# Attention beside a mixture of experts: score operands stored once, transfers two at a time, work moved off VectorE

## The chip, the core and the metric

The kernel runs on one core of a Trainium2 chip. The metric is the device time of one execution in microseconds; a profiled execution adds a span (first to last instruction) and a trace. TensorE, VectorE, ScalarE and GpSimd compute; SP only issues DMAs. All float data is fp32.

## The reference

x has 8 batches of 512 rows of 128 channels. It is normalised (xn), and the output is x + attention(xn) + experts(xn).

```python
q, k, v = (xn @ w.T + b  for wq, wk, wv)          # 16 heads of 8 channels
scores  = where(xn[:, :, 0] != 0, q k^T * 8**-0.5, -inf)
att     = softmax(scores) @ v @ wo.T + bo

logits  = xn @ gate_w                              # 4096 rows, 8 experts
top 2 per row, router_probs = softmax of the two
rank of each (choice, row) within its expert; kept if rank < 1280
slots   = kept rows of xn, gathered by (expert, rank)
y       = gelu(slots @ c_fc[e] + fc_bias[e]) @ c_proj[e] + proj_bias[e]
ffn     = sum over the two choices of weight * y[slot]
```

## The kernel before, in words

Every engine runs a list of instructions written out by hand; semaphores are the only order between engines. The stages are these.

**Front.** For each of the 8 batches the rows are normalised (VectorE), transposed (TensorE), and multiplied by the weights of q and k. Both are split into a high part, rounded to the fast fp32 format of TensorE (`high` on ScalarE), and a low part, the rest (`late` on VectorE). The score product is then formed from 24 rows per head: K's (low, high, high) against Q's (high, high, low), three rows for each of 8 channels. `write_stacks` on SP stores these triples to `q_rows` and `k_rows` in HBM, with four DMAs a batch; a high part may be overwritten two batches later only when its stores have landed (`s_wr`). GpSimd adds the bias of v and stores a mask row to `k_rows`.

**Preparation.** VectorE picks the two best experts; GpSimd turns ranks into slots (`put_i`, `get_i`, weights `wgt`). TensorE meanwhile forms the first scores for the maxima and, between them, filler products (`keep_clock`). GpSimd then adds the output bias to `acc` in one instruction, fills `slot_x` with zeros by ten DMAs, one at a time, and scatters the rows of xn to their slots by 64 indirect DMAs, each released at a group of attention (`put_after`).

**Attention.** A batch has 16 groups: two units of 8 heads, each as two quads of 4 heads, times 4 blocks of 128 keys. In a group TensorE forms four transposed scores (line 967), each followed by an exponential on ScalarE (line 621), four products of the group before with v (line 983), and, eight groups ahead, two pairs of scores (line 948) whose row maxima VectorE takes (line 765). Every four groups, here called a quarter, SP loads the stacks of one quad of the next batch (`load_quad`, 8 DMAs) and, behind them on the same queue, writes the maxima of a quad into rows of Q (`max_rows`, 4 DMAs); these were turned by TensorE in the second group of a quarter and are needed at the first group of the next. In the first groups of a batch the previous batch is normalised, turned, projected with wo (line 1002) and added to `acc` (`take_out`).

**Experts.** They run after four groups of batch 4. For each expert TensorE turns the slot rows `xe` (line 991), forms the first product from split parts (lines 1059 to 1063) and the second (line 1074), with the turning of the next expert's rows woven in as `BETWEEN` says: two chunks of rows, a result, the last chunk of rows, two results. VectorE writes `ye`, SP stores it to `slot_y`. SP's order per expert is: wait for the rows of e to be split, load rows of e + 1, wait for the results of e, store them, load the weights of e + 2.

**Combining.** GpSimd gathers each row's two results from `slot_y` by 64 indirect DMAs, again released at groups (`got_after`). Batches 0 to 3 are combined by GpSimd, 4 to 6 by VectorE between maxima (line 830, at the groups in `COMBINED_AT`), batch 7 by VectorE at the end. SP writes each batch out.

## Time and profile before

| | us |
|---|---|
| median of 3 runs | 714.14 |
| lowest, highest | 707.48, 723.22 |
| profiled execution | 716.14 |
| its span | 714.3 |
| TensorE busy | 618.3 (87%) |
| VectorE busy | 406.7 (57%) |
| ScalarE busy | 394.9 (55%) |
| GpSimd busy | 229.0 (32%) |
| chain that ended last | TensorE 52%, VectorE 21%, DMA 8%, ScalarE 6% |

The profile divides the span by engine and by line. A busy share says little about what bounds, since matmuls overlap in the array; the waits (who sat idle, and what ended that) and the chain of work that ended last say more. The granted clock of TensorE has two levels here, 1.2 and 2.4 GHz, shown as 0.5 and 1.0 of full speed.

### The profile page before, as it was taken

How to read it: one execution, taken by the hardware profiler on the slowest of the kernel's cores; microseconds unless marked ns; L12 is line 12 of the kernel's file. 1: busy time of each engine (PE TensorE's matmuls, PEld its weight loads, DVE VectorE, ACT ScalarE, POOL GpSimd, SP SyncE). 2: the span in 40 equal slices, each digit the busy share in tenths (PEclk: the TensorE clock that was granted, in tenths of full speed). 3: DMA queues.
4: the chain of work that ended last, by engine and by line, in shares of the span. 5: the costliest groups of instructions: out<-in, count | busy, mean ns of one | idle time of the engine just before them, and what ended most of it. 6: DMA issues, size and time to landing. Idle time of an engine off the chain costs nothing.

```text
span 714.3 us, 9757 instructions
## 1 busy us (share of the span) xinstructions
PE 618.3 (87%) x3526; PEld 322.6 (45%) x3526; DVE 406.7 (57%) x601; ACT 394.9 (55%) x775; POOL 229.0 (32%) x230
## 2 busy tenths in 40 slices
PE   4767999599999999989778867969999999899884
PEld 2433443223333343358767766869334333224312
DVE  5758598458888979831111110111798988857602
ACT  3442067357778877883144134323877787655751
POOL 3856911623343431200110011010255566322310
PEclk9989599759999999999789989889999999756955
DMA  6887044211212121422133033211312122111120
GB/s 191 248 277 233 21 180 155 72 38 51 73 54 74 59 68 39 119 67 74 34 107 104 27 84 108 64 45 38 102 47 76 48 73 80 58 43 27 47 66 15
DMA packets 57999, 60.44 MB, mean 85 GB/s; under 512 B 8032, under 2 KB 42848, under 8 KB 57952
## 3 DMA queue, kind: packets, MB, share of 16 engines
q1 hardware_dynamic: 52160, 45.92, 21.3%
q0 software_dynamic: 5792, 13.90, 6.3%
q8 instruction: 28, 0.46, 0.3%
q14 instruction: 19, 0.16, 0.1%
HBM read 29.65 MB, written 29.62 MB: 83 GB/s over the span
## 4 chain that ended last, share of the span: by engine, by line
PE 52%; DVE 21%; DMA 8%; ACT 6%; SPq 5%; issue 4%; POOL 1%; another core or an unknown queue 1%; DVEq 0%; POOLq 0%; ACTq 0%
DVE nmax L765 14%; PE bPV L983 14%; PE bX L967 12%; PE bD L1074 12%; DMA xe<-slot_x 5%; PE bD L948 5%; ACT probs L621 4%; PE bPV L1109 2%; PE bX L957 2%; DMA k_rows<-hid 2%; PE bD L991 1%; PE bD L1002 1%; DVE ye L808 1%; SPq L368 1%; DVE attn L783 1%
## 5 line engine op out<-in xcount | busy, mean ns | idle before, releaser
L765 DVE TENSOR_REDUCE nmax<-bD 128x2 f32<-128x1024 f32 x256 | 300.5, 1218 | 76.5 <-PE bD L948 58.7
L621 ACT ACTIVATE probs<-bX 128x512 f32<-128x512 f32 x512 | 268.2, 597 | 114.7 <-PE bX L967 102.6
L967 PE MATMUL bX<-Q,K 27*128 27x512 f32 x512 | 186.4, 503 | 19.0 <-ACT probs L621 12.6
L983 PE MATMUL bPV<-probs,v_aug 128*32 128x512 f32 x1024 | 152.0, 668 | 1.6 <-ACT probs L621 0.7
L967 PEld LDWEIGHTS bX<-Q,K 27*128 27x128 f32 x512 | 76.0, 196 | 163.5 <-ACT probs L621 111.3
L948 PE MATMUL bD<-K,Q 25*128 25x512 f32 x512 | 137.2, 508 | 10.7 <-DVE nmax L765 7.4
L1074 PE MATMUL bD<-wpj,hid 128*128 128x128 f32 x640 | 88.2, 306 | 11.4 <-DVE xeT_lo L798 6.3
L1074 PEld LDWEIGHTS bD<-wpj,hid 128*128 128x128 f32 x640 | 85.8, 220 | 14.8 <-issue 14.8
L512 POOL DMA_INDIRECT slot_x<-xn_all,put_i x64 | 62.4, 975 | 90.3 <-PE bPV L983 76.4
L649 ACT ACTIVATE hid<-bX,fcb 128x512 f32<-128x512 f32 (+1 forms) x96 | 55.5, 615 | 47.1 <-PE bX L1063 46.5
L948 PEld LDWEIGHTS bD<-K,Q 25*128 25x128 f32 x512 | 58.6, 197 | 47.1 <-DVE nmax L765 29.8
L519 POOL TENSOR_TENSOR wfc_hi<-wfc,ones 128x512 fp32r<-128x512 f32 x8 | 10.1, 1265 | 175.4 <-DMA pjb<-in_pjb 175.4
L808 DVE TENSOR_TENSOR ye<-bD,pjb 128x512 f32<-128x512 f32 (+1 forms) x24 | 14.5, 603 | 84.2 <-PE bD L1074 84.2
L798 DVE TENSOR_TENSOR xeT_lo<-bD,xeT_hi 128x512 fp32r<-128x512 f32 (+1 forms) x24 | 13.9, 597 | 80.1 <-ACT xeT_hi L646 80.1
L542 POOL DMA_INDIRECT xn_all<-slot_y,get_i x32 | 32.2, 1005 | 69.8 <-PE bPV L983 65.1
L542 POOL DMA_INDIRECT hid<-slot_y,get_i x32 | 32.0, 999 | 64.7 <-PE bPV L983 54.9
L646 ACT CAST xeT_hi<-bD 128x512 fp32r<-128x512 f32 (+1 forms) x24 | 11.9, 517 | 67.5 <-PE bD L991 67.5
L983 PEld LDWEIGHTS bPV<-probs,v_aug 128*32 128x32 f32 x1024 | 21.3, 112 | 38.9 <-ACT probs L621 23.2
L1059 PE MATMUL bX<-xeT_hi,wfc_lo 128*128 128x512 f32 (+1 forms) x96 | 35.1, 366 | 0.7 <-ACT hid L649 0.7
L1063 PE MATMUL bX<-xeT_lo,wfc_hi 128*128 128x512 f32 (+1 forms) x96 | 34.2, 357 | 0.0
L1060 PE MATMUL bX<-xeT_hi,wfc_hi 128*128 128x512 f32 (+1 forms) x96 | 34.1, 355 | 0.0
L991 PE MATMUL bD<-ident,xe 128*128 128x128 f32 x80 | 14.5, 323 | 22.5 <-DMA xe<-slot_x 21.5
(104 smaller groups left out, 488.3 us busy)
## 6 DMA issues: line engine op xcount, KB each, us to landing
K<-k_rows SPq DMA_DIRECT2D x128, 50.0 KB
Q<-q_rows SPq DMA_DIRECT2D x128, 48.0 KB
slot_x<-hid POOLq DMA_DIRECT2D x10, 512.0 KB, 3.0
xe<-slot_x SPq DMA_DIRECT2D x8, 640.0 KB, 6.3
slot_y<-ye SPq DMA_DIRECT2D x8, 640.0 KB, 4.3
q_rows<-hid SPq DMA_DIRECT2D x8, 512.0 KB, 3.7
k_rows<-hid SPq DMA_DIRECT2D x8, 512.0 KB, 5.4
acc<-in_x SPq DMA_DIRECT2D x8, 256.0 KB, 4.9
```

The lines of the kernel that those rows point to most:

```text
L512: pool.indirect_dma_start(slot_x, bass.IndirectOffsetOnAxis(ap=put_i[:, col:col + 1], axis=0), xn_all[:, n, :], None, bounds_check=SLOTS - ...
L542: pool.indirect_dma_start(gathered(b, k * TT + n), None, slot_y, bass.IndirectOffsetOnAxis(ap=get_i[:, col:col + 1], axis=0), bounds_check ...
L621: taken(nc.scalar.activation(probs[:, (g % 2) * 4 + i, :], next_x()[:], ACT.Exp, scale=SCALE))
L649: taken(nc.scalar.activation(hid[:, hc, c0:c0 + w], next_x()[:, 0:w], ACT.Gelu, bias=fcb_s[q][:, hc:hc + 1]))
L765: nc.vector.tensor_reduce(nmax[q][:, k, 2 * pair:2 * pair + 2], bank()[:], AX.X, ALU.max, negate=True).then_inc(s_dd, 1)
L948: last = nc.tensor.matmul(to[:, n, :], Q[u][rows_used, q, k * P:(k + 1) * P], K[u][rows_used, q, :], start=True, stop=True)
L967: filled(nc.tensor.matmul(next_x()[:], K[u][rows_used, q, j * P:(j + 1) * P], Q[u][rows_used, q, :], start=True, stop=True))
L983: last = nc.tensor.matmul(bPV[32 * h:32 * h + 32, :], v_aug[b % 2][:, j, u * UH + QUAD * q + h, :], probs[:, (g % 2) * 4 + h, :], start=(g ...
L1059: nc.tensor.matmul(to, lo, xeT[0][:, c0:c0 + w], start=True, stop=False)
L1060: nc.tensor.matmul(to, hi, xeT[0][:, c0:c0 + w], start=False, stop=False)
L1063: filled(nc.tensor.matmul(to, hi, xeT[1][:, c0:c0 + w], start=False, stop=True))
L1074: last = nc.tensor.matmul(to[:, 0, k * P:(k + 1) * P], hid[:, hc, c0 + k * P:c0 + (k + 1) * P], wpj[e % 2][:, hc, :], start=(hc == 0), sto ...
```

## The change

Eight things change. (1) `q_rows` and `k_rows` hold, for each channel, one high and one low row; two stores a batch write them, and `load_quad` makes the triples by reading the high row of Q twice: four DMAs a head instead of two. (2) The stores of batches 0 to 5 stand ahead of the first load. (3) Zero stores, scatters and gathers wait for the one two before them, on a pair of semaphores, and for no group. (4) The output bias is added in eight pieces, one after every second of the first sixteen scatters. (5) SP loads the rows of expert e + 2 ahead of the wait for the results of e. (6) Batches 4 to 6 are combined by GpSimd behind the last gather. (7) The first filler row on TensorE after the ranks has 8 products instead of 3. (8) In the last eight groups, where no scores for maxima are left, TensorE forms two pairs of score products that nobody reads.

```diff
-HI, LO = (1, 0), (0, 1)
+HI, LO = 1, 0
...
-COMBINED_BY_POOL = 4
+COMBINED_BY_POOL = 7
 N_CONST, N_LATER = 8, 3
-WR_DMAS, LOAD_DMAS, MAX_DMAS = 4, 8, 4
+WR_DMAS, LOAD_DMAS, MAX_DMAS = 2, 16, 4
...
+def taken_out(b):
+
+    return D_FIRST + (b + 1) * D_TURN + (E * D_EXPERT if b > EXPERTS_AFTER else 0)
...
-        q_rows = nc.dram_tensor("q_rows", [B, H, ROW_MASK, T], F32, kind="Internal").ap()
-        k_rows = nc.dram_tensor("k_rows", [B, H, ROW_MAX, T], F32, kind="Internal").ap()
+        q_rows = nc.dram_tensor("q_rows", [B, H, DH, 2, T], F32, kind="Internal").ap()
+        k_rows = nc.dram_tensor("k_rows", [B, H, DH + 1, 2, T], F32, kind="Internal").ap()
...
                 sp.wait_ge(s_lo, b * 2 + 2)
                 for w, stack in ((0, q_rows), (1, k_rows)):
-                    three = stack[b, :, 0:ROW_MASK, :].rearrange("h (c r) t -> h c (r t)", r=3)
-                    sp.dma_start(three[:, :, 0:2 * T], parts[w, q].rearrange("p s t -> p (s t)")).then_inc(s_wr[b], 16)
-                    sp.dma_start(three[:, :, 2 * T:3 * T], parts[w, q][:, HI[w], :]).then_inc(s_wr[b], 16)
+                    sp.dma_start(stack[b, :, 0:DH].rearrange("h c s t -> h c (s t)"), parts[w, q].rearrange("p s t -> p (s t)")
+                                 ).then_inc(s_wr[b], 16)
 
             def load_quad(b, u, q):
 
@@ -333,9 +326,13 @@
                     sp.wait_ge(s_wr[b], WR_DMAS * 16)
                     sp.wait_ge(s_wm[b % 2], b // 2 * 16 + 16)
                 for h in range(QUAD):
-                    for tile, stack, n in ((Q[u], q_rows, ROW_MASK), (K[u], k_rows, ROW_MAX)):
-                        sp.dma_start(tile[STRIP * h:STRIP * h + n, q, :].bitcast(F32), stack[b, h0 + h]
-                                     ).then_inc(s_load[u][q], 16)
+                    at = STRIP * h
+                    for start, stop, tile, src in (
+                            (0, 2 * DH, Q[u], q_rows[b, h0 + h, :, HI, :][None, :, :].to_broadcast([2, DH, T])),
+                            (2 * DH, ROW_MASK, Q[u], q_rows[b, h0 + h, :, LO, :]),
+                            (0, 2 * DH, K[u], k_rows[b, h0 + h, 0:DH].rearrange("c s t -> s c t")),
+                            (2 * DH, ROW_MAX, K[u], k_rows[b, h0 + h, :, HI, :])):
+                        sp.dma_start(tile[at + start:at + stop, q, :].bitcast(F32), src).then_inc(s_load[u][q], 16)
 
...
-            for b in range(3):
+            for b in range(B - 2):
                 write_stacks(b, b % 2)
             sp.wait_ge(s_ones, 2 * UNITS)
             load_quad(0, 0, 0)
-            for b in range(3, 6):
-                write_stacks(b, b % 2)
+            write_stacks(B - 2, 0)
+            write_stacks(B - 1, 1)
             load_quad(0, 0, 1)
-            for b in range(6, B):
-                write_stacks(b, b % 2)
-                load_quad(0, 1, b % 2)
+            for q in range(2):
+                load_quad(0, 1, q)
...
             def experts():
-                sp.wait_ge(s_put, KN * 16)
+                for q in range(2):
+                    sp.wait_ge(s_put[q], KN // 2 * 16)
                 load_rows(0)
+                sp.wait_ge(s_dd, rows_item(0, NCH - 1) + 1)
+                load_rows(1)
                 for e in range(E):
-                    if e < E - 1:
-                        sp.wait_ge(s_dd, rows_item(e, NCH - 1) + 1)
-                        load_rows(e + 1)
+                    if e + 2 < E:
+                        sp.wait_ge(s_dd, rows_item(e + 1, NCH - 1) + 1)
+                        load_rows(e + 2)
                     sp.wait_ge(s_dd, results_end(e))
                     sp.dma_start(slot_y_v[e], ye[:]).then_inc(s_slot, 16)
...
-                    take_pool(2, COMBINED_BY_POOL)
+                    take_pool(2, 4)
...
+            take_pool(4, COMBINED_BY_POOL)
...
-            pool.wait_ge(s_xn, B)
-            nc.gpsimd.tensor_tensor(acc[:], acc[:], bo_s[:, None, :].to_broadcast([P, NT, C]), ALU.add).then_inc(s_bo, 1)
             pool.wait_ge(s_fill, 7)
             for h in range(ZERO_DMAS):
                 pool.dma_start(slot_x.rearrange("(p h r) c -> h p (r c)", p=P, h=ZERO_DMAS)[h], hid_f[:, 0:per]
-                               ).then_inc(s_zero, 16)
-                pool.wait_ge(s_zero, h * 16 + 16)
+                               ).then_inc(s_zero[h % 2], 16)
+                wait(pool, s_zero[1 - h % 2], (h + 1) // 2 * 16)
+            pool.wait_ge(s_xn, B)
+            pool.wait_ge(s_zero[(ZERO_DMAS - 1) % 2], ZERO_DMAS // 2 * 16)
             for k in range(TOPK):
                 for n in range(NT):
                     col = k * NT + n
-                    pool.wait_ge(s_pv, put_after(col))
+                    wait(pool, s_put[col % 2], col // 2 * 16)
                     pool.indirect_dma_start(slot_x, bass.IndirectOffsetOnAxis(ap=put_i[:, col:col + 1], axis=0),
                                             xn_all[:, n, :], None, bounds_check=SLOTS - 1, oob_is_err=False
-                                            ).then_inc(s_put, 16)
+                                            ).then_inc(s_put[col % 2], 16)
+                    if col < 2 * B and col % 2 == 1:
+                        b = col // 2
+                        nc.gpsimd.tensor_tensor(rows(acc, b), rows(acc, b), bo_s[:, None, :].to_broadcast([P, TT, C]),
+                                                ALU.add).then_inc(s_bo, 1)
             for e in range(E):
...
+                for q in range(2):
+                    pool.wait_ge(s_get[b][q], TOPK * TT // 2 * 16)
+                pool.wait_ge(s_dd, taken_out(b))
...
-                        pool.wait_ge(s_pv, got_after((b * TOPK + k) * TT + n))
+                        if k * TT + n >= 2:
+                            pool.wait_ge(s_get[b][n % 2], (k * TT + n) // 2 * 16)
+                        elif b > 0:
+                            pool.wait_ge(s_get[b - 1][n % 2], TOPK * TT // 2 * 16)
                         pool.indirect_dma_start(gathered(b, k * TT + n), None, slot_y,
                                                 bass.IndirectOffsetOnAxis(ap=get_i[:, col:col + 1], axis=0),
-                                                bounds_check=SLOTS - 1, oob_is_err=False).then_inc(s_get[b], 16)
-                        if 0 < b <= COMBINED_BY_POOL and (k, n) == (0, 2):
+                                                bounds_check=SLOTS - 1, oob_is_err=False).then_inc(s_get[b][n % 2], 16)
+                        if 0 < b <= EXPERTS_AFTER + 1 and (k, n) == (0, 2):
                             combine(b - 1)
+            for b in range(EXPERTS_AFTER + 1, COMBINED_BY_POOL):
+                combine(b)
...
-                dve.wait_ge(s_bo, 1)
+                dve.wait_ge(s_bo, b + 1)
...
-                if b * GB + g in COMBINED_AT:
-                    combine(COMBINED_AT[b * GB + g])
...
+            def unused_products():
+
+                to = free()
+                for n in range(2):
+                    at = STRIP * n
+                    nc.tensor.matmul(to[:, n, :], Q[1][at:at + NR_MAX, 1, 0:P], K[1][at:at + NR_MAX, 1, :], start=True, stop=True)
...
+                    else:
+                        unused_products()
...
-                        keep_clock(3)
+                        keep_clock(8 if (s, pair) == (2, 0) else 3)
```

Three places show what moves. On SP, at the start of the experts; `xe` are slot rows, `ye` results, the rest weights. Before:

```order
L345 DMA Q<-nmT 2x512 x4
L363 DMA xe<-slot_x 128x10x128 x2
L380 DMA slot_y<-ye 128x10x128
L367 DMA wfc<-in_c_fc 128x512
L368 DMA wpj<-in_c_proj 128x4x128
L369 DMA fcb<-in_fcb 128x4
L370 DMA pjb<-in_pjb 128x128
L363 DMA xe<-slot_x 128x10x128
L380 DMA slot_y<-ye 128x10x128
```

After:

```order
L342 DMA Q<-nmT 2x512 x4
L359 DMA xe<-slot_x 128x10x128 x3
L379 DMA slot_y<-ye 128x10x128
L363 DMA wfc<-in_c_fc 128x512
L364 DMA wpj<-in_c_proj 128x4x128
L365 DMA fcb<-in_fcb 128x4
L366 DMA pjb<-in_pjb 128x128
L359 DMA xe<-slot_x 128x10x128
L379 DMA slot_y<-ye 128x10x128
```

The load of the third expert's rows now stands ahead of the first store of results, and so on for each expert.

On VectorE, batch 6, groups 6 to 10; `nmax` are row maxima, line 830 the combine. Before:

```order
L771 TENSOR_TENSOR nmhl<-nmax,nmhl 128x16
L765 TENSOR_REDUCE nmax<-bD 128x2 x4
L779 RECIPROCAL rsum<-bD 128x32
L783 TENSOR_TENSOR attn<-bD,rsum 128x4x32 x2
L830 SCALAR_TENSOR_TENSOR acc<-hid,wgt,acc 128x128 x8
L765 TENSOR_REDUCE nmax<-bD 128x2 x4
L770 CAST nmhl<-nmax 128x16
L771 TENSOR_TENSOR nmhl<-nmax,nmhl 128x16
```

After:

```order
L784 TENSOR_TENSOR nmhl<-nmax,nmhl 128x16
L778 TENSOR_REDUCE nmax<-bD 128x2 x4
L792 RECIPROCAL rsum<-bD 128x32
L796 TENSOR_TENSOR attn<-bD,rsum 128x4x32 x2
L778 TENSOR_REDUCE nmax<-bD 128x2 x4
L783 CAST nmhl<-nmax 128x16
L784 TENSOR_TENSOR nmhl<-nmax,nmhl 128x16
```

The combine is gone from between the maxima.

On TensorE, the last batch, around its eighth group; `bX` takes scores for exponentials, `bD` scores for maxima. Before:

```order
L983 MATMUL bPV<-probs,v_aug 32x512 x4
L967 MATMUL bX<-Q,K 128x512
L957 MATMUL bX<-ident,nmhl 8x128 x4
L967 MATMUL bX<-Q,K 128x512 x3
L983 MATMUL bPV<-probs,v_aug 32x512 x4
L991 MATMUL bD<-ident,pv_s 128x128 x4
L967 MATMUL bX<-Q,K 128x512 x4
L983 MATMUL bPV<-probs,v_aug 32x512 x4
```

After:

```order
L1003 MATMUL bPV<-probs,v_aug 32x512 x4
L987 MATMUL bX<-Q,K 128x512
L977 MATMUL bX<-ident,nmhl 8x128 x4
L987 MATMUL bX<-Q,K 128x512
L970 MATMUL bD<-K,Q 128x512 x2
L987 MATMUL bX<-Q,K 128x512
L970 MATMUL bD<-K,Q 128x512 x2
L987 MATMUL bX<-Q,K 128x512
L1003 MATMUL bPV<-probs,v_aug 32x512 x4
L1011 MATMUL bD<-ident,pv_s 128x128 x4
L987 MATMUL bX<-Q,K 128x512 x2
L970 MATMUL bD<-K,Q 128x512 x2
```

Each group has two pairs of products more, in the places that the scores for maxima have in earlier groups.

## Rows read from the trace of the kernel before

**Rows 1.** The page, section 2: granted clock in 40 equal slices

```profile
PEclk9989599759999999999789989889999999756955
```

**Rows 2.** Waits, whole run: total us, times, longest us

```profile
PEld bD L991 <- DMA xe<-slot_x: 22.8, 6, 4.1
...
ACT hid L557 <- DMA k_rows<-hid: 20.9, 6, 5.1
...
ACT probs L621 <- remote: 6.8, 2, 6.4
```

**Rows 3.** Timeline of the front, ScalarE and GpSimd: start us, us, what [idle before]

```profile
21.43 0.69 ACT L557 ACTIVATE hid<-bX,bq_s 128x512 fp32r<-128x512 f32 x1 [1.73 <-DMA k_rows<-hid]
...
54.39 0.69 ACT L557 ACTIVATE hid<-bX,bq_s 128x512 fp32r<-128x512 f32 x1 [2.33 <-DMA k_rows<-hid]
...
30.18 1.92 POOL L446 TENSOR_SCALAR mrow<-ye 1x512 fp32r<-1x512 f32 x1
...
34.34 1.92 POOL L446 TENSOR_SCALAR mrow<-ye 1x512 fp32r<-1x512 f32 x1
```

**Rows 4.** Timeline of the preparation, TensorE: filler products between pairs

```profile
80.07 1.65 PE L1109 MATMUL bPV<-hot,ones_r 128*128 128x512 f32 x3
...
82.37 1.65 PE L1109 MATMUL bPV<-hot,ones_r 128*128 128x512 f32 x3
...
89.33 0.96 PE L1109 MATMUL bPV<-hot,ones_r 128*128 128x512 f32 x3
...
90.64 0.96 PE L1109 MATMUL bPV<-hot,ones_r 128*128 128x512 f32 x3
```

**Rows 5.** Timeline of TensorE, experts 0 and 1

```profile
319.22 1.04 PE L991 MATMUL bD<-ident,xe 128*128 128x128 f32 x8
...
326.23 5.60 PE L1074 MATMUL bD<-wpj,hid 128*128 128x128 f32 x48 [0.73 <-DVE ye L808]
...
342.51 1.97 PE L991 MATMUL bD<-ident,xe 128*128 128x128 f32 x8 [3.70 <-DMA xe<-slot_x]
```

**Rows 6.** The chain of waits: start us, us, what

```profile
260.05 1.10 PE bD L1002 x8
...
307.39 1.09 PE bD L1002 x8
...
362.52 6.29 DMA xe<-slot_x
...
479.31 5.60 PE bD L1074 x48
...
547.15 1.10 PE bD L1002 x8
...
657.15 1.10 PE bD L1002 x8
```

**Rows 7.** Timeline of VectorE, batch 6

```profile
614.06 2.31 DVE L830 SCALAR_TENSOR_TENSOR acc<-hid,wgt,acc 128x128 f32<-128x128 f32 x8
```

**Rows 8.** Timeline of TensorE, last batch

```profile
680.15 1.94 PE L983 MATMUL bPV<-probs,v_aug 128*32 128x512 f32 x8
...
684.21 1.94 PE L983 MATMUL bPV<-probs,v_aug 128*32 128x512 f32 x8
```

**Rows 9.** Timeline of SP's queue, two quarters of batch 2

```profile
237.03 0.30 SPq L337 DMA_DIRECT2D Q<-q_rows  x1
...
248.05 0.29 SPq L337 DMA_DIRECT2D Q<-q_rows  x1
...
250.44 0.30 SPq L337 DMA_DIRECT2D K<-k_rows  x1
251.84 2.41 SPq L345 DMA_DIRECT2D Q<-nmT  x4
```

**Rows 10.** DMA queues, 213.9 to 224.9 us (one quarter): packets, MB, share

```profile
q1 hardware_dynamic: 280, 0.42, 11.8%
```

**Rows 11.** DMA issues: count, KB each, median us to landing

```profile
bk_s<-in_bk SPq DMA_DIRECT2D x1, 0.5 KB, 2.1
```

29 lines of the change are left out of this document (13 added, 16 removed).

## The prediction

> **What bounds the kernel now.** I read the page's slices first, then the waits, then the chain that ended last, and at each place where the chain names something other than TensorE or the maxima on VectorE, the timeline there. The clock slices [rows 1] say where to look: TensorE's granted clock is at its upper level, 2.4 GHz, in most slices and falls to half, 1.2 GHz, in the preparation (slice 5), in slices 8 and 9, in a part of every expert (the 7 and the 8s of slices 20 to 27), and in five of the last six. A group of attention costs 11.0/4 = 2.76 us at the upper level ([rows 9]: loads of consecutive quarters start at 237.03 and 248.05) and 4.06 us at the lower [rows 8], because TensorE then needs longer than the two maxima on VectorE. So a short pause of TensorE costs its own length and then 1.3 us per group until the clock is back. Three pauses are visible: the exponentials that wait for stored stacks in the front, the expert rows that wait for their load [rows 2], and one pause of 6.4 us on an unnamed releaser near 135 us [rows 2].
>
> **The change, part by part.** The sum is made against the profiled execution, 716.1 us (span 714.3, 1.8 outside it), which lies 2.0 over the median of the runs.
>
> *Front.* Stores shrink from four DMAs of 1,536 KB per batch to two of 1,024 KB, and no load stands between them before batch 5. ScalarE waited 20.9 us in six waits for a store two batches back [rows 2]; the high parts of batches 2 and 7 are 54.39 − 21.43 = 32.96 us apart, 6.6 per batch [rows 3]. Without that wait the next limit is GpSimd's mask, store and bias of a batch, 34.34 − 30.18 = 4.16 us [rows 3]. Five intervals at 4.16 are 20.8 us: a gain of at most 12. Against it, the first load is now issued behind six batches and takes sixteen DMAs, so it may reach TensorE up to 5 us after the front's end. I take **−8**, bounds −12 and −3.
>
> *Preparation.* TensorE runs 12 pairs of score products after the ranks, at 82.37 − 80.07 = 2.30 us a pair at the lower clock, and at 90.64 − 89.33 = 1.31 at the upper [rows 4]. Ahead of the first it now issues 8 filler products instead of 3: three take 1.65 us [rows 4], so 5 more take 2.8. If this denser stretch of work lifts the clock after two or three pairs, 9 pairs save 1.0 us each, −9 + 2.8 = −6.2; if not, +2.8. No row shows eight in a row from this state; I take **−3.5**, the middle, leaning to a gain, since in the experts the clock came back each time once full 128-row products ran.
>
> *GpSimd's queue.* The bias of the output (acc plus bo) leaves its place ahead of the zero stores and is cut in eight pieces among the first sixteen scatters; zero stores and scatters go two at a time, held only by their own landing. The scatters had been spread over four batches, so that without the spreading they end long before the experts read the slots; each of the eight pieces precedes its take-out by many groups. TensorE waits for none of it: **0**. The pause near 135 us falls into a run of scatters issued back to back, but its releaser is not named; I leave it at 0, bounds −15 (6.4 of pause, some 2 of slow issue before it, and five groups that then ran at 4.06, 5 × 1.3) and +15 (a second such).
>
> *Experts.* This is the largest term. SP issues the next load of expert rows behind the last result, its store and four weight loads; it takes 6.29 us [rows 6], and TensorE, done with the first products, waits 3.70 us [rows 5], six times, 22.8 us [rows 2]. After each the clock falls. Periods: the last 12 chunks of results start at 326.23 [rows 5] and 479.31 [rows 6], so (479.31 − 326.23)/6 = 25.5 us. An undisturbed period is built from the same rows: 326.23 − 319.22 = 7.0 (rows to the second result) plus 342.51 − 3.70 − 326.23 = 12.6 (results and first products) = 19.6. The load now goes out once the third chunk of rows is split, ahead of the last two results; these and the first products, the 12.6 us above, cover 6.3. (25.5 − 19.6) × 6 = **−36**. If the clock fell all the same, the pauses alone give −22. Cover: if a load took over 12 us, TensorE would wait again. What is late next is the weight split on GpSimd, which has a whole expert of time.
>
> *Combines on VectorE.* Three leave VectorE for GpSimd's end. The one at 614.06 takes 2.31 us [rows 7] between maxima; TensorE's banks are full, and the clock stays low for ten groups. Batches from 260.05 to 307.39 take 47.3; two from 547.15 to 657.15 take 110.0 [rows 6]: 110.0 − 94.7 = **−15.3**. All of it should return, as nothing else stands there. On GpSimd three combines of four passes each run behind the last gather, and only batch 6's has to wait for a take-out, which comes 12 groups before the end: hidden.
>
> *Unused products.* In the last eight groups TensorE repeats the score pairs for nobody. It fell to 4.06 us per group at about 680 [rows 8]; five groups at 2.76 give −6.5, and the closing transposes and projection, all at the lower clock too, perhaps −2. Cost of the added products: in all other groups they fit in 2.76. **−8.5**, bounds 0 and −11.
>
> *Loads.* Each quarter's load becomes 16 DMAs on SP instead of 8, and the maxima rows (4 DMAs) stand behind them. Eight take 250.44 − 248.05 + 0.30 = 2.7 us, 0.34 each; the maxima's four are issued in 2.41 [rows 9], and a small DMA lands 2.1 after issue [rows 11]. From the load's first issue T, the maxima rows land at T + 16 × 0.34 + 1.8 + 2.1 = T + 9.3; TensorE needs them a quarter later, T + 11.0. Cover 1.7 us, so **0**. Bounds: the issue cost of the new shapes is between 0.34 and the 0.60 of the maxima's two-row DMAs (2.41/4); from 0.44 on, TensorE waits.
>
> How many engines a load uses can be read off its small packets: in one quarter 280 packets of which 204 are rows [rows 10]; the other 76 are 4 × 12 + 4 × 5 + 4 × 2, so 24 rows went over 12 engines, 25 over 5, 2 over 2. The Trainium skill, DMA: Bandwidth & Descriptors, "Why a DMA increments its semaphore by 16 and not by 1", gives the rule: the count is the largest number up to 16 that divides the slowest dimension of both sides, on the lowest-numbered engines; by it the two new 16-row forms, whose slowest dimension is 2, would use two engines. By that rule the trace agrees for the old shapes; for the new ones (16 rows twice over 2, 8 over 8, 9 over 9) it would put 4 × (8 + 8 + 1 + 1) = 72 rows of a quarter on each of two engines, against 28 so far, with the maxima rows behind them, and the cover of 1.7 would shrink to about nothing. The sum stands without it.
>
> Sum: −8 − 3.5 − 36 − 15.3 − 8.5 = −71.3; 716.1 − 71.3 = **645 us**.
>
> **Rivals.** (a) *The pause near 135 us goes too*: 645 − 15 = 630. For it: the scatters beside it had no wait on a landing; against: scatters land fast enough that two in flight is the same pace. (b) *Maxima rows late by about 1 us* in each of the 31 quarters, clock unharmed: 645 + 31 = 676. For it: the 1.7 us of cover, and GpSimd's transfers, now at full pace beside them. (c) *Slower: the same wait drops the clock.* From an issue cost over 0.44 us, TensorE pauses at each quarter's head; where the pause comes near the 2.3 us of the combine [rows 7], the shortest that a fall followed, a batch runs some 12 of 16 groups at 4.06: 96 low groups in place of the 20 of before (5, 10 and 5 above), 76 × 1.3 = +99, and 716 − 47.5 + 99 = 768. A low clock makes the quarter long enough for the loads, so it settles there and no deeper. (d) *The change does not hold the clock*: the fillers bring +2.8 and the unused products nothing: 645 + 6.3 + 8.5 = 660. For it: no row shows score products alone bringing a fallen clock back; against: the full attention groups consist mostly of them and keep the upper level.
>
> **How the numbers follow.** The forecast 0.58, (a) 0.13, (b) 0.12, (c) 0.09, (d) 0.08. The forecast's own bounds are 630 to 662. The range goes from 622 (a and a better front) to 690 (b with some fallen clocks); only (c) and a little beyond lie outside. A measurement of this kernel can tell about 2% from no change: under 700 faster, over 728 slower. Faster 0.84, same 0.06, slower 0.10.
>
> **What would show it.** In the changed profile: no wait on the expert rows' load, and a clock slice of 9 through the experts, one in 19 to 20 us; high parts 4 to 5 us apart in the front; no low clock in the last three batches; the maxima rows' last issue no later than 8 us after their quarter's first load. Wrong would be: waits of the score products on the maxima rows, load issues of 0.45 us or more, or low slices inside the attention batches, which say (b) or (c); 2.30 us pairs to the end of the preparation, which say (d).

## The result, and the profile after

The change makes the kernel **slower**: 765.6 us median (754.3 to 775.3), against 713.1 of before, ratio 1.068 (95% interval 1.047 to 1.088). The profiled execution took 764.1 us, its span 762.3. Ratios here compare quick executions with quick ones, since a clock that falls by chance makes single executions longer; medians and ranges are given beside them, and the kernel before always ran on the same chip.

The clock slices come first again, from the page of the changed kernel (section 2):

```profile
PEclk9989655569559657855999999999556855977996
```

Against [rows 1], the experts (slices 20 to 28) are all 9 now, and the attention before and behind them is at 5 and 6 in long stretches where it was 9. So one part gave what it should, and something else took far more. The waits of the changed kernel (total us, times, longest us) name it:

```profile
PE bX L987 <- DMA Q<-nmT: 22.2, 7, 10.2
...
ACT hid L570 <- DMA k_rows<-hid: 6.8, 4, 2.7
```

TensorE waits for the maxima rows, which it never did before; the wait on `xe` [rows 2] is gone, and the wait for a store in the front fell from 20.9 to 6.8 us. Seven waits of 22 us in all don't make the 48 us by which the span grew. What they do is seen where one ends. SP's queue and TensorE at the head of the third quarter of batch 3, two timelines of the changed kernel:

```profile
304.02 1.09 SPq L335 DMA_DIRECT2D Q<-q_rows  x2
305.15 1.08 SPq L335 DMA_DIRECT2D K<-k_rows  x2
...
312.92 2.42 SPq L342 DMA_DIRECT2D Q<-nmT  x4
315.38 1.09 SPq L335 DMA_DIRECT2D Q<-q_rows  x2
```

```profile
313.50 1.07 PE L1003 MATMUL bPV<-probs,v_aug 128*32 128x512 f32 x8
314.49 0.50 PE L987 MATMUL bX<-Q,K 27*128 27x512 f32 x1
316.51 0.49 PE L987 MATMUL bX<-Q,K 27*128 27x512 f32 x1 [1.52 <-DMA Q<-nmT]
316.95 0.43 PE L987 MATMUL bX<-Q,K 27*128 27x512 f32 x2
317.31 1.94 PE L1003 MATMUL bPV<-probs,v_aug 128*32 128x512 f32 x8
```

Two things are to be seen here. The first is the cost of an issue, the time that SP spends on starting one DMA: a pair takes 1.09 us, and the next starts 0.04 later, so 0.56 an issue, where [rows 9] had 0.34. Sixteen take 8.9 us and the maxima's four 2.4, so SP is busy for 11.3 us of a quarter that lasts 11.0 at the upper clock. The maxima rows land 1.1 us after their last issue, at 316.5, 12.5 after the quarter's first load. TensorE had been ready at 315.0. The second is the clock: behind the pause of 1.52 us the eight products with v take 1.94 us instead of 1.07, so it has fallen.

In batches 1 to 6 it fell in this way at the head of the third quarter, and once more at the head of batch 7, behind a pause of 1.57 us at 697.1. In batch 0 it was low from the start, behind the wait of 10.2 us. In batch 1 the pause is 1.16 us and the table names no releaser for it; it ends at 187.3, 1.1 us behind the last maxima issue, as the others do. In batches 1 to 5 the clock came back only at the next batch's head, with its products of 128 rows; batch 6 fell at 669.5 and had it back at 677.7, behind such products too. Batch lengths, from the first score product of one batch to that of the next (us):

| | b0 | b1 | b2 | b3 | b4 with experts | b5 | b6 |
|---|---|---|---|---|---|---|---|
| before | 55.9 | 51.2 | 47.3 | 47.4 | 239.7 | 47.3 | 57.0 |
| after | 67.5 | 65.1 | 64.5 | 64.3 | 222.5 | 64.5 | 57.5 |

The front and the preparation, ScalarE and TensorE of the changed kernel:

```profile
20.81 0.69 ACT L570 ACTIVATE hid<-bX,bq_s 128x512 fp32r<-128x512 f32 x1 [1.08 <-PE bX L902]
...
42.55 0.69 ACT L570 ACTIVATE hid<-bX,bq_s 128x512 fp32r<-128x512 f32 x1 [2.69 <-DMA k_rows<-hid]
```

```profile
50.29 0.80 PE L961 MATMUL bD<-K,Q 25*128 25x512 f32 x4 [7.46 <-DMA K<-k_rows]
...
59.71 2.11 PE L1130 MATMUL bPV<-hot,ones_r 128*128 128x512 f32 x8 [0.73 <-ACT wpj L601]
...
64.29 0.96 PE L1130 MATMUL bPV<-hot,ones_r 128*128 128x512 f32 x3
65.18 0.50 PE L961 MATMUL bD<-K,Q 25*128 25x512 f32 x2
65.61 0.96 PE L1130 MATMUL bPV<-hot,ones_r 128*128 128x512 f32 x3
...
77.83 1.20 PE L1130 MATMUL bPV<-hot,ones_r 128*128 128x512 f32 x4
89.19 0.79 PE L987 MATMUL bX<-Q,K 27*128 27x512 f32 x1 [10.17 <-DMA Q<-nmT]
```

High parts of batches 2 and 7 are now (42.55 − 20.81)/5 = 4.35 us apart instead of 6.6 [rows 3]. The preparation runs at 1.32 us a pair from its start, where [rows 4] had 2.30 for the most part, and is done at 79.0. Then TensorE waits 10.2 us, because the first maxima rows stand behind 64 load issues on SP.

The experts, chain of waits (start us, us, what), the last twelve chunks of results:

```profile
385.79 5.60 PE bD L1096 x48
405.21 5.60 PE bD L1096 x48
...
482.90 5.60 PE bD L1096 x48
```

The period is (482.90 − 385.79)/5 = 19.4 us, against 25.5 [rows 5], [rows 6]. The spans can be compared by segments. The attention starts at 89.2 instead of 93.1: −3.9. From the last products with v ahead of the experts to the first behind them it is 159.1 instead of 195.7: −36.6. All other attention takes 514.0 instead of 425.5: +88.5. Together that is +48.0, by which the spans differ.

### The profile page after: what moved, and what is told of

It reads as the page before. It is cut to its first block, busy times and chain, and to the rows that moved or that the text cites. A ratio compares the mean times of both kernels' runs of the same rounds, so it can differ in the third digit from the quotient of the medians.

```text
span 762.3 us, 10070 instructions
## 1 busy us (share of the span) xinstructions
PE 674.6 (88%) x3563; PEld 319.2 (42%) x3563; DVE 403.5 (53%) x577; ACT 396.0 (52%) x775; POOL 244.3 (32%) x249
## 4 chain that ended last, share of the span: by engine, by line
PE 64%; ACT 13%; DVE 9%; SPq 7%; issue 4%; DMA 2%; DVEq 0%; ACTq 0%
PE bPV L1003 22%; PE bX L987 19%; PE bD L1096 10%; ACT hid L662 6%; SPq L335 5%; ACT probs L634 5%; PE bD L961 4%; DVE nmax L778 4%; PE bX L977 3%; PE bD L1011 2%; DMA Q<-nmT 2%; SPq L342 1%; PE bD L1022 1%; DVE xn_all L713 1%; DVE hid L722 1%
## 5 line engine op out<-in xcount | busy, mean ns | idle before, releaser
L987 PE MATMUL bX<-Q,K 27*128 27x512 f32 x512 | 224.3, 615 | 35.5 <-DMA Q<-nmT 22.2
L1003 PE MATMUL bPV<-probs,v_aug 128*32 128x512 f32 x1024 | 199.0, 861 | 0.8 <-ACT probs L634 0.7
L987 PEld LDWEIGHTS bX<-Q,K 27*128 27x128 f32 x512 | 92.8, 244 | 234.1 <-ACT probs L634 106.9
L961 PE MATMUL bD<-K,Q 25*128 25x512 f32 x512 | 150.0, 614 | 13.5 <-DMA K<-k_rows 7.5
L1096 PE MATMUL bD<-wpj,hid 128*128 128x128 f32 x640 | 74.9, 277 | 13.5 <-DVE xeT_lo L811 8.4
L1096 PEld LDWEIGHTS bD<-wpj,hid 128*128 128x128 f32 x640 | 72.6, 192 | 16.4 <-issue 16.4
L961 PEld LDWEIGHTS bD<-K,Q 25*128 25x128 f32 x512 | 61.8, 247 | 34.9 <-issue 15.6
L1003 PEld LDWEIGHTS bPV<-probs,v_aug 128*32 128x32 f32 x1024 | 23.3, 126 | 48.0 <-ACT probs L634 26.0
L617 ACT CAST nmT<-bX 8x512 fp32r<-8x512 f32 x32 | 18.4, 574 | 21.4 <-PE bX L977 19.4
L977 PE MATMUL bX<-ident,nmhl 128*8 128x128 f32 x128 | 28.3, 365 | 0.1
```

The costliest lines, as they stand in the source:

```text
L961: last = nc.tensor.matmul(to[:, n, :], Q[u][rows_used, q, k * P:(k + 1) * P], K[u][rows_used, q, :], start=True, stop=True)
L977: last = nc.tensor.transpose(to[0:8, k * P:(k + 1) * P], nmhl[q][:, k, :, :].rearrange("p h s -> p (h s)").bitcast(F32), ident[:])
L987: filled(nc.tensor.matmul(next_x()[:], K[u][rows_used, q, j * P:(j + 1) * P], Q[u][rows_used, q, :], start=True, stop=True))
L1003: last = nc.tensor.matmul(bPV[32 * h:32 * h + 32, :], v_aug[b % 2][:, j, u * UH + QUAD * q + h, :], probs[:, (g % 2) * 4 + h, :], start=(g ...
L1096: last = nc.tensor.matmul(to[:, 0, k * P:(k + 1) * P], hid[:, hc, c0 + k * P:c0 + (k + 1) * P], wpj[e % 2][:, hc, :], start=(hc == 0), sto ...
```

## The experiments

Each kernel is given by its difference from another. "On old stacks" means the first one below. The letters of theories and rivals are those of the expectations.

### Is it the loads?

**Old stacks.** All of the change, but the layout, stores and loads of before (part 1 undone):

```diff
-WR_DMAS, LOAD_DMAS, MAX_DMAS = 2, 16, 4
+WR_DMAS, LOAD_DMAS, MAX_DMAS = 4, 8, 4
...
-                            (0, 2 * DH, Q[u], q_rows[b, h0 + h, :, HI, :][None, :, :].to_broadcast([2, DH, T])),
...
+                    for tile, stack, n in ((Q[u], q_rows, ROW_MASK), (K[u], k_rows, ROW_MAX)):
+                        sp.dma_start(tile[STRIP * h:STRIP * h + n, q, :].bitcast(F32), stack[b, h0 + h]
```

> The changed kernel with the operand stacks of the kernel before: triples stored, eight loads of 24 and 25 rows a quarter. Theory A (SP's issue time: sixteen issues at 0.55 us and the maxima's four take 11.3 us of a quarter of 11.0, TensorE pauses at the quarter's head and its clock falls): the load's issues go back to 2.7 us a quarter, no wait on the maxima rows, batches of 47.3 us, and the other seven parts keep what they bring: 645 to 655. Rival B (the unpaced scatters and gathers, or the combines at GpSimd's end, slow the transfers or TensorE): batches stay well over 50 us and the time over 690.

Measured: 658.5 us median (642.5 to 660.2; before, on this chip, 715.9). No wait on the maxima rows is left; batches 2, 3, 5 and 6 take 47.3 to 48.0. Batch 0 ran at the lower clock throughout in the profiled execution, 66.8 us, from 86.8 on and with no pause of TensorE of 0.3 us or more in the 8 us ahead, which the page shows as slices 6 to 10:

```profile
PEclk9988965555999999999999999999999999999997
```

**The loads alone**, on the kernel before:

> The kernel before with the new stacks and their sixteen loads alone. Theory A: batches of some 64.5 us as in the changed kernel, and none of the other gains: the changed kernel's 765 plus 36.6 of the experts plus some 8 of the last groups, 800 to 815. Rival B: the loss needs the unpaced transfers, so this one stays within 2% of 714.

Measured: 814.7 us (804.0 to 820.1), ratio 1.135 (1.115 to 1.155). Seven waits again, and batches of 62 to 69 us, with the scatters still spread as before:

```profile
PE bX L970 <- DMA Q<-nmT: 16.8, 7, 3.3
```

So part 1, the new layout with its stores and loads, is necessary and sufficient: with it alone the loss is there, and where it alone is undone the loss is gone.

**Pairs.** The sixteen rows channel by channel, so that K's lie in one piece:

```diff
-                            (0, 2 * DH, Q[u], q_rows[b, h0 + h, :, HI, :][None, :, :].to_broadcast([2, DH, T])),
+                            (0, 2 * DH, Q[u], q_rows[b, h0 + h, :, HI, :][:, None, :].to_broadcast([DH, 2, T])),
...
-                            (0, 2 * DH, K[u], k_rows[b, h0 + h, 0:DH].rearrange("c s t -> s c t")),
+                            (0, 2 * DH, K[u], k_rows[b, h0 + h, 0:DH].rearrange("c s t -> (c s) t")),
```

> The changed kernel with the sixteen rows of Q and K ordered channel by channel in pairs, so that K's sixteen rows lie in one piece in HBM. If the issue cost follows the pieces of the address pattern, K's sixteen-row issue falls from 0.60 to 0.30 and Q's stays at 0.61: mean pitch 0.48, the maxima rows land 16 x 0.48 + 3.6 = 11.3 us after the quarter's first load, 0.3 late. Theory A with a graded effect: pauses of 0.3 us, too short to cost the clock, about 655 to 665. Theory A with any pause costing the clock: 740 to 765. Rival C (two DMA engines carry the sixteen-row loads and hold up the maxima rows): the rows spread over more engines, maxima land sooner after their issue than 1.1 us and that alone mends it.

Measured: 716.7 us (688.7 to 726.3; before 715.9), between the two expectations. SP's timeline of that kernel, one quarter:

```profile
283.43 1.22 SPq L335 DMA_DIRECT2D Q<-q_rows  x2
284.69 0.69 SPq L335 DMA_DIRECT2D K<-k_rows  x2
...
290.57 1.96 SPq L335 DMA_DIRECT2D K<-k_rows  x2
292.58 2.46 SPq L342 DMA_DIRECT2D Q<-nmT  x4
```

K's pair of issues went from 1.08 to 0.69, Q's rose from 1.08 to 1.22. This quarter has one issue that is 1.3 us longer than its like, and such single long issues decide: the maxima rows landed at 296.2, 12.7 us after the first load and 1.2 after their own last issue. By rival C the number of DMA engines should have mattered. Here the form uses eight and sixteen of them, and a quarter has 365 packets where the changed kernel has 296; the rows landed as soon behind their last issue as in the changed kernel. So what was late was the issue, not the transfer.

The pause is graded, and its price is not. With the clock at the upper level ahead of it, pauses of 0.2 to 0.8 us at a quarter's head (four in this kernel, one in the next) left it there. The pauses from 1.2 to 3.3 us in the changed kernel, the loads alone and these two were 19; every one was followed by groups at the lower level, 12 of them to the end of the batch. Away from a quarter's head shorter pauses were followed by a fall too: 0.95 us in this kernel, at 186.0, and 0.68 and 0.77 in two kernels below.

**Old stacks, each load cut in two** plain DMAs of 12 and 12 or 13 rows:

```diff
+                        for start, stop in ((0, 12), (12, n)):
+                            sp.dma_start(tile[STRIP * h + start:STRIP * h + stop, q, :].bitcast(F32),
+                                         stack[b, h0 + h, start:stop]).then_inc(s_load[u][q], 16)
```

> The old stacks, but each load of 24 or 25 rows cut into two DMAs of 12 and 12 or 13 rows: sixteen DMAs a quarter of plain contiguous rows. Prediction's assumption (0.34 us an issue whatever the count) puts 5.4 + 3.6 = 9.1 us before the maxima rows are there, inside 11.0: time as with eight loads, 645 to 655. If the number of DMAs by itself costs (0.55 each even for plain rows): 750 to 770.

Measured: 707.8 us (689.7 to 721.1; before 715.9), so neither. This is the prediction's assumption built: sixteen plain loads. A pair of them takes 0.77 us, and now and then 1.0 more:

```profile
258.47 0.77 SPq L332 DMA_DIRECT2D Q<-q_rows  x2
259.28 1.79 SPq L332 DMA_DIRECT2D K<-k_rows  x2
261.11 2.41 SPq L340 DMA_DIRECT2D Q<-nmT  x4
```

At 0.41 an issue four batches kept their 47 to 52 us, but the 64 issues in the preparation made TensorE wait 4.1 us for the first maxima, and batches 0 and 1 then took 67.5 and 65.1. The fall in batch 1, at 194.1, isn't behind a maxima wait: it follows pauses of 0.51, 0.94 and 0.32 us without a named releaser, while GpSimd's scatters ran. By the medians (658 with eight plain loads, 708 with sixteen, 766 with sixteen of the new forms) the number of DMAs and their form each have a large part in the loss. Single executions of each kernel spread by 18 to 31 us, so the split is rough.

### What are the other parts worth?

**Three fillers** on old stacks (part 7 undone: `keep_clock(3)` everywhere):

> The changed kernel with the old stacks, and three filler products after the ranks instead of eight (part 7 undone). Theory D (the eight fillers bring the clock to its upper level for the preparation, but the attention that follows then loses it at its start and runs batch 0 at the lower level: 66.8 us instead of some 50): with three the preparation runs at 2.30 us a pair, batch 0 starts at the upper level as in the kernel before, and the time is 645 to 650 in every run, below the 658 of the run with old stacks alone. Rival E (batch 0's fall has nothing to do with the fillers): the preparation gets slower by some 6 us and batch 0 is low as often as before: 650 to 668.

Measured: 644.5 us (638.2 to 662.1), ratio 0.926 (0.908 to 0.943). The profiled execution started its attention 8 us later than with eight fillers (91.4 against 83.4) and ran batch 0 in 44.7. But one execution of four took 662, and a kernel with eight fillers (combines on VectorE, below) ran its batch 0 in 43.9. So theory D is not settled. In none of the four profiles with three fillers (the kernel before, the loads alone, this one, and the kernel before with two in flight) did batch 0 start low. With eight fillers and no wait for the first maxima it did in three of eleven. The execution of 662 has no profile, so where it lost its time isn't known.

**Fillers in the first groups** of batch 0, eight pairs of 128-row products on old stacks:

```diff
+                if b == 0 and LEAD <= u * UH + s < LEAD + 4:
+                    for n in range(2):
+                        nc.tensor.matmul(to[:, n, :], ones_r[:], hot_f, start=True, stop=True)
```

> The changed kernel with the old stacks, and two filler products of 128 rows ahead of each pair of score products in the first four groups of batch 0 (16 in all, whose results nobody reads). Theory F (batch 0 falls because its first groups have too little work in TensorE after the dense preparation, and full 128-row products keep or bring back the clock, as the turned sums did at the head of batch 1): batch 0 takes 50 to 55 us instead of 66.8, cost of the fillers some 2 to 4 us, 642 to 650 in every run. Rival: batch 0 low all the same, 660 to 665.

Measured: 642.4 us (639.0 to 648.5), ratio 0.929 (0.918 to 0.941), as theory F had it. It did not hold: see the same kernel again, below.

**Two in flight in the kernel before** (scatters held also by the landing of the one two before):

> The kernel before, with the 64 scatters held in addition by the landing of the one two before them; nothing else changed. Theory G (the pause of 6 us near 135 us comes from a dozen scatters issued back to back without a wait for a landing): no pause, batch 0 some 10 to 15 us shorter, time 700 to 706. Rival: the pause comes from something else at that place (it stays, or moves), and the time is that of the kernel before.

Measured: 700.0 us (694.3 to 718.1) against 704.5 (690.2 to 731.1), ratio 1.006 (0.999 to 1.013). In the profile the pause is gone and batch 0 takes 43.8 us instead of 55.9; the times show no gain. Since the kernel before itself ran in 690 here, its pause was perhaps not in every execution, or not at that price; no profile shows which.

**Combines on VectorE** again, on old stacks (part 6 undone):

> The changed kernel with the old stacks, but batches 4 to 6 combined by VectorE between maxima as in the kernel before (part 6 undone). By the prediction's term the three combines cost 15.3 us: 3 x 2.3 us at least, and a fallen clock after the one near the end: 658 plus 7 to 15. If the fall before was chance, plus 7 only or nothing.

Measured: 649.1 us (642.8 to 670.9), ratio 0.936 (0.922 to 0.950). VectorE and TensorE of that kernel where a combine stands:

```profile
555.87 2.32 DVE L844 SCALAR_TENSOR_TENSOR acc<-hid,wgt,acc 128x128 f32<-128x128 f32 x8
```

```profile
559.37 0.50 PE L963 MATMUL bD<-K,Q 25*128 25x512 f32 x2 [1.44 <-DVE nmax L778]
...
561.17 1.60 PE L1005 MATMUL bPV<-probs,v_aug 128*32 128x512 f32 x8
```

The same 1.4 us pause stood behind the combine near the end of the kernel before, where eight groups ran low behind it. Here the clock falls too, but for two groups only: the three groups from 556.43 to 569.65 take 13.2 us, against 8.4 in batch 5, so 4.9 more. A second combine at the head of batch 7 cost 2.7, the third nothing.

**No unused products**, on old stacks with the fillers in batch 0 (part 8 undone):

> The kernel with old stacks and fillers in batch 0's first groups, without the unused products of the last eight groups (part 8 undone). Theory H (they hold the clock to the end): the last four groups and the closing products run at the lower level, +6 to +9 us, 649 to 651. Rival: the clock holds or falls there either way, within 2 us of 642.

Measured: 674.4 us (660.2 to 683.2; before 712.9), ratio 0.936 (0.923 to 0.950). The time can't be read as expected, since batches 1 and 2 lost the clock on this chip without any quarter's wait. Both falls stand behind a pause of TensorE while scatters ran, 1.44 us at 148.0 and 0.68 at 206.7. At the first, ScalarE, VectorE and GpSimd went on within 0.05 us of one another (148.67 to 148.72), though the products that ScalarE is said to wait for had ended by 148.0. So the releasers named here need not be the cause:

```profile
148.67 2.15 ACT L631 ACTIVATE probs<-bX 128x512 f32<-128x512 f32 x4 [1.88 <-PE bX L987]
149.45 0.50 PE L961 MATMUL bD<-K,Q 25*128 25x512 f32 x2 [1.44 <-DVE acc L800]
```

The end can be read. TensorE's last products with v, of this kernel and of the changed one:

```profile
655.26 1.94 PE L1003 MATMUL bPV<-probs,v_aug 128*32 128x512 f32 x8
659.33 1.94 PE L1003 MATMUL bPV<-probs,v_aug 128*32 128x512 f32 x8
```

```profile
742.87 1.07 PE L1003 MATMUL bPV<-probs,v_aug 128*32 128x512 f32 x8
745.47 1.07 PE L1003 MATMUL bPV<-probs,v_aug 128*32 128x512 f32 x8
747.64 1.94 PE L1003 MATMUL bPV<-probs,v_aug 128*32 128x512 f32 x8 [0.69 <-ACT probs L634]
```

From the tenth group's products with v to the last it is 22.3 us here and 15.2 in the changed kernel: 7.1 us. Without the unused products the clock fell in the tenth or eleventh group of 16 in all four profiles (the kernel before, the loads alone, the kernel before with two in flight, and this one). With them it held to the end in four (old stacks, fillers in the groups, and spread scatters with the stacks stored twice or K once); there the span ended 12.8 to 12.9 us behind the last products with v instead of 14.6, which is 1.8 more. In the changed kernel and six others it was lost in the last one or two groups all the same, and in the three kernels whose clock was low through batch 7 the unused products did not bring it back.

**The old order of the expert loads**, on the same base (part 5 undone):

> The kernel with old stacks and fillers in batch 0's first groups, and SP's order in the experts as before the change (part 5 undone). By the prediction's term: 3.7 us waits on the rows of the next expert six times and a low clock behind each, period 25.5 instead of 19.4, +36: 677 to 680. If the other parts had a share in that gain, less.

Measured: 704.7 us (689.8 to 723.0; before 712.9), ratio 0.976 (0.965 to 0.987). The wait is back, and so is the period, (461.70 − 334.02)/5 = 25.5 us:

```profile
PE bD L1009 <- DMA xe<-slot_x: 21.9, 6, 3.8
```

```profile
334.02 5.61 PE bD L1094 x48
...
461.70 5.61 PE bD L1094 x48
```

Its group with the experts takes 195.6 us, from products with v to products with v, against 159.1 in the kernel without unused products on the same chip: 36.4.

This kernel also shows a price of combining on GpSimd that the prediction doesn't have. VectorE, GpSimd and TensorE at a combine:

```profile
651.75 1.87 DVE L778 CAST nmhl<-nmax 128x16 fp32r<-128x16 f32 x1
651.54 2.04 POOL L533 TENSOR_TENSOR hid<-hid,wgt 128x512 f32<-128x512 f32 x2
654.48 0.61 PE L959 MATMUL bD<-K,Q 25*128 25x512 f32 x2 [1.40 <-DVE acc L798]
```

The CAST takes 0.18 us where it stands alone. Beside GpSimd's combine it takes 1.87 and ends with it, TensorE comes to wait 1.40 us, and the clock is low from 654.7 for 68.5 us. The same stands ahead of a fall in five more kernels on old stacks or with K once, with an instruction of VectorE of 1.3 to 2.7 us and pauses of TensorE of 0.3 to 1.0 us. One of them is the kernel with combines on VectorE, where GpSimd has only those of batches 0 to 3, as before the change. In three others such a long instruction had no fall behind it. So the combine on GpSimd frees VectorE's own time and can still hold VectorE up. That it causes these falls is argued from the rows; no run takes it apart.

### What do the scatters do?

**Scatters free**: not held by landings at all, same base:

```diff
-                    wait(pool, s_put[col % 2], col // 2 * 16)
```

> The kernel with old stacks and fillers in batch 0's first groups, with the 64 scatters not held by anything but their issue. Theory G (a dozen unheld scatters in a row pause the engines some 6 us and drop the clock): from the tenth to the fifteenth scatter on, a pause of 3 to 7 us on an unnamed releaser on TensorE, ScalarE and GpSimd, a low clock behind it, 652 to 665. Rival (the pause near 135 us had another cause): no pause, 642 as with two in flight.

Measured: 724.6 us (703.6 to 747.0; before 712.9), worse than either. ScalarE's timeline and GpSimd's in that kernel:

```profile
165.44 0.60 ACT L630 ACTIVATE probs<-bX 128x512 f32<-128x512 f32 x1 [20.46 <-remote]
169.09 0.60 ACT L630 ACTIVATE probs<-bX 128x512 f32<-128x512 f32 x1 [3.05 <-remote]
177.46 0.60 ACT L630 ACTIVATE probs<-bX 128x512 f32<-128x512 f32 x1 [7.78 <-remote]
...
197.09 0.60 ACT L630 ACTIVATE probs<-bX 128x512 f32<-128x512 f32 x1 [12.04 <-remote]
```

```profile
187.79 0.97 POOL L508 DMA_INDIRECT slot_x<-xn_all,put_i  x1 [0.31 <-issue]
189.07 0.97 POOL L508 DMA_INDIRECT slot_x<-xn_all,put_i  x1 [0.30 <-issue]
```

While GpSimd issues a scatter every 1.28 us without a wait, ScalarE sits idle 57 us in eight waits with the unnamed releaser of [rows 2], and the first two groups of batch 1 take 60.9 us. The last of these stops ends 8 us behind the last scatter. That is the pause near 135 us of the kernel before, made larger: there the scatters ran unheld for some 17 us.

**Spread and held**, with three beside it on one chip. The kernel with old stacks and fillers again (the reference); scatters also spread over groups as before the change; gathers too, up to group 104; and K stored once, Q in triples, with twelve loads a quarter and spread scatters. The last had run before, with scatters not spread:

> The kernel with old stacks and fillers in batch 0's first groups, but K's operands stored once and loaded in two DMAs a head (sixteen contiguous rows of high and low pairs, then nine high rows), Q's stored in triples and loaded in one: twelve loads a quarter. By the issue times seen, 0.30, 0.31 and 0.33, with 0.04 between: 12 x 0.36 + 3.6 = 7.9 us from the quarter's first load to the maxima rows' landing, inside 11.0, so no pause and no low clock in the batches; the front stores 2.5 MB a batch instead of 3 and starts the preparation 1 to 3 us earlier: 638 to 643. If long single issues eat the cover as with sixteen plain loads: pauses at the third quarter's head and 650 to 700.

Measured: 685.9 us (672.0 to 688.1; before 712.9), on the chip on which the three kernels beside it lost the clock in batch 1 too. Its issues were as worked out, 0.32, 0.35 and 0.33 us, apart from single ones of 1.57. Its clock fell at 134.5 us, in the middle of the scatters, behind a pause of TensorE of 2.13 us. ScalarE stood still with it:

```profile
134.75 2.08 ACT L635 ACTIVATE probs<-bX 128x512 f32<-128x512 f32 x4 [2.77 <-remote]
```

It is the pause of the kernel before in small, with two scatters in flight. VectorE of the kernel with the old expert order, on the same chip, has one of 1.8 us in batch 1, and its clock fell there too.

> The kernel with old stacks and fillers in batch 0's first groups, with each scatter held as before the change by a group of attention, beside its hold by the landing of the one two before. Theory J (64 scatters at full pace from 97 to 190 us delay semaphores by 1 to 2 us now and then and so drop the clock in batches 1 and 2): no low clock there in the profile, and a time below that of the same kernel without the spreading on the same chip, by 5 to 25 us where that one has falls. Rival (the chip): both have the same falls and the same time within 1%.

> The kernel with old stacks and fillers in batch 0's first groups once more, as the reference on this chip for the three beside it. Theory J: 640 to 675, with falls in batches 1 and 2 where the time is high. Rival (the chip): the same as its three neighbours.

> As the kernel with spread scatters, with the gathers spread over the groups up to group 104 as well. If gathers at full pace cost as scatters do: no low clock in batches 5 and 6, 2 to 10 us below the kernel with spread scatters alone. If not: the same, or up to 3 us more where the last combine comes too late.

> K's operands stored once and twelve loads a quarter, with spread scatters. By the issue times, 7.9 us to the landing of the maxima rows inside 11.0: with the scatters out of the way no falls, and 1 to 3 us below the kernel with old stacks and spread scatters, by the shorter front. If twelve loads are too many by themselves (single issues of 1.5 us on top): falls at the third quarter of some batches and 10 to 30 us above it.

| | median | range | ratio | low clock in the profile |
|---|---|---|---|---|
| reference again | 639.9 | 637.3 to 674.2 | 0.910 (0.898 to 0.923) | batch 0, batch 7 |
| spread scatters | 643.5 | 635.5 to 656.9 | 0.910 (0.893 to 0.928) | first four groups of batch 0 |
| spread scatters and gathers | 643.2 | 638.1 to 647.4 | 0.915 (0.901 to 0.929) | last two groups |
| K once, spread | 644.3 | 634.4 to 669.5 | 0.907 (0.893 to 0.922) | batches 4 and 5 |

The four can't be told apart in time, and with scatters at full pace batches 1 and 2 kept the clock here. Theory J, that scatters at full pace cost the clock, has only the profiles for it. Of the eleven kernels with two scatters in flight at full pace, five have pauses of TensorE of 0.7 to 2.1 us in that stretch that no quarter explains (the pairs, each load in two, K once, no unused products, and the old expert order), and the clock falls behind them. The other six have none and no such fall. Of the four with spread scatters (the kernel before with two in flight among them) none has either. Five of eleven against none of four is too few to settle it. All four beat the kernel before by 8.5 to 9.3%. Fillers don't prevent a fall, as the reference shows. TensorE, batch 0's first groups:

```profile
90.30 0.50 PE L961 MATMUL bD<-K,Q 25*128 25x512 f32 x2
...
90.95 1.93 PE L1003 MATMUL bPV<-probs,v_aug 128*32 128x512 f32 x8
92.81 0.79 PE L987 MATMUL bX<-Q,K 27*128 27x512 f32 x2
```

Between the last row at full speed and the first at half there is no idle time at all.

## Why the prediction was wrong

The step that failed is in *Loads*: "Eight take 250.44 − 248.05 + 0.30 = 2.7 us, 0.34 each", carried over to sixteen DMAs of other shapes, with "Cover 1.7 us, so **0**". The bounds stood there, 0.34 to the 0.60 of the two-row DMAs, and the point from which TensorE waits, 0.44; the value taken was the lower end. Measured: 0.61 for a sixteen-row issue, 0.42 for one of eight or nine rows, 0.56 on the mean from start to start. So the maxima rows landed 8.9 + 2.4 + 1.1 = 12.5 us behind the first load, where 9.3 was reckoned and a quarter lasts 11.0. The row that should have been trusted was the two-row one in [rows 9]: it moves a twelfth of the bytes of its neighbours and costs twice as much, so size doesn't set the cost, and a form that no row shows belongs near the dear end. What does set it is only partly known: K's nine rows cost 0.42 in the changed kernel and 0.33 in the pairs kernel, by the same DMA behind another neighbour. From the last load issue to the landing the prediction had 3.9 us; it was 2.5 + 1.1 = 3.6. By that the deciding point is (11.0 − 3.6)/16 = 0.46, and even plain loads at 0.41 come too near it.

**Rival (c)** is what happened: the same wait drops the clock. It gave 768 us by 76 more low groups at 1.3, on a base of 716 − 47.5; 765.6 came out. The mechanism was right, and that the number is so near is partly luck. The profiles have 72 low groups against 18, so 54 more, and the pauses, which the rival left out, take some 13 us on top; the attention outside the experts lost 88.5 us by both. The start and the experts gave 40.5, not 47.5. The rows of before could have warned that a short pause is enough: the prediction takes 2.3 us of VectorE's combine as the shortest that a fall followed, but TensorE itself had stood still for only 1.40 us there, and for 1.08 at 133.9. The other reading of the same loads, that few DMA engines carry them, can be checked in the packets of one quarter, 269.8 to 282.4 us (queue: packets, MB, share):

```profile
q1 hardware_dynamic: 296, 0.42, 10.9%
```

204 of the 296 are rows, as in [rows 10], and 92 are left: 4 × (2 + 2 + 8 + 9) + 4 × 2. So the sixteen-row forms do use two engines each. By the rule cited in the prediction (the Trainium skill, DMA: Bandwidth & Descriptors, "Why a DMA increments its semaphore by 16 and not by 1") the trace agrees to the packet. It doesn't bind: the maxima rows landed 1.1 us behind their last issue here, and 1.2 in the pairs kernel, whose loads use more engines.

**Front**, −8 forecast. The high parts came 4.35 us apart (4.16 forecast) and the last one 11.8 earlier. TensorE then waited 7.5 us for the first load, and the first fillers stand 5.2 earlier (59.71 against 64.95). Right in kind, 3 too much. With the old stacks, where the high parts are 6.0 us apart again, the first fillers stand at 64.1, only 0.8 earlier: so most of this gain is the smaller stores' and goes with the loads that cost more.

**Preparation**, −3.5 forecast. From the first filler to the last it took 19.3 us instead of 28.1: −8.8, beyond the bound of −6.2. The clock did not have to come back after two or three pairs, for it never left. But the 10.2 us of waiting for the first maxima rows took it all; the sum had priced the loads of the quarters and not the 64 issues ahead of batch 0.

**GpSimd's queue**, 0 with a rival of −15. In fifteen profiles with scatters two in flight no pause of 6 us is left, the longest that has no named releaser is 2.8, and with unheld scatters it grew to 57 us. So the mechanism of rival (a) is shown; that it gains time isn't, with 1.006 for the kernel that has this part alone.

**Experts**, −36 forecast: 36.6 in the changed kernel, 36.4 when the order is put back.

**Combines**, −15.3 forecast. The pause of 1.4 us is there in both kernels; how many groups run low behind it varies: eight in the kernel before, where the prediction counted ten, and two in the experiment, where all three cost 7.6 together. By one profile each it can't be said what sets the number. And the combine on GpSimd, put at no cost, held VectorE up in places, as shown above.

**Unused products**, −8.5 forecast: the groups gave 7.1 (6.5 forecast), the closing products 1.8 (2 forecast) where the clock held to the end, and nothing in the changed kernel, where it fell in the last groups.

Without the loads the total comes to what was forecast: 645 by the sum, and 640 to 645 by the medians on two chips, but 658.5 for the first kernel on old stacks, and 674 and 686 on a third chip. In part that is luck, since errors cancel: the front gave 0.8 and not 8 there, the preparation 8.8 and not 3.5, and the pause near 135 us, put at 0, is gone. The experts and the unused products were priced well. The term put at nothing cost 765.6 − 658.5 = 107 us.

**What stays open.** Why the clock falls with no pause ahead of it, in batch 0 of three kernels on old stacks and in the last groups of three others; how far scatters at full pace, with pauses of TensorE of 0.7 to 2.1 us among them, add to the falls; how far the combine on GpSimd does; and what sets the cost of an issue beyond its form.

## What to carry to other kernels

A queue that issues DMAs has a time budget per period like any engine: sum its issues, each by a row of the same form, and where no row has the form, build and time one before relying on it. A layout that saves bytes in HBM but doubles the issues moves the cost from a place with slack to one without. Where a clock falls behind a pause of a little over a microsecond, the margin of a wait is worth far more than the wait: leave cover for one long issue as well, not for the mean only. And work that is moved to an idle engine can still hold up the one that it was taken from: compare the durations of that engine's instructions beside it.

## What the runs showed of the hardware

- An issue on SP took 0.30 to 0.32 us for 24 contiguous rows of 2 KB, 0.31 to 0.35 for 16 contiguous, 0.36 for 12 or 13, 0.33 to 0.46 for 8 or 9 rows at every second row (0.42 in the changed kernel), 0.60 to 0.69 for sixteen rows as two sets of eight, and 0.56 to 0.60 for two rows between tiles; 0.04 lies between two. Single issues took 0.9 to 1.6 us in the attention and up to 2.5 in the preparation. The same DMA of nine rows took 0.42 or 0.33 in kernels that differ in its neighbours.
- Indirect stores issued without waiting for any to land stopped ScalarE for up to 20 us at a time, 57 us in all; with two in flight the longest stop without a named releaser was 2.8 us.
- At the head of a quarter of attention, pauses of TensorE up to 0.8 us left the clock at 2.4 GHz, and all 19 of 1.2 us and more were followed by 1.2 GHz. Elsewhere in the attention pauses of 0.68 to 0.95 us were followed by it too, and six falls had no pause of 0.3 us or more in the 8 us ahead. In the experts, pauses of 1.2 us between full products left it at 2.4.
- A CAST of VectorE that takes 0.18 us alone took 1.87 us beside a TENSOR_TENSOR pair of GpSimd, and ended with it.
